# Splitting all feed-forward weights and rotary tables during the first attention, kept in DRAM

## The reference

```python
x1 = x  + attn(layernorm(x), W_Q, W_K, W_V, W_O)      # causal, 16 heads of 64
x2 = x1 + xattn(layernorm(x1), ctx, mask, ...)        # linear attention, 16 heads of 16
y  = layernorm(x2)
for l in range(2):                                    # DEPTH
    h = shift_token(y); q, k, v = split(h @ wqkv[l], 3)      # 8 heads of 64
    q, k = l2norm(q) * q_scale[l], l2norm(k) * k_scale[l]
    q, k = rotary_xpos(q, k)                          # cos, sin and scale tables
    y = y + local_attention(q, k, v) @ wo[l]          # windows of 128
    a, g = split(layernorm(shift_token(y)) @ w1[l] + b1[l], 2)
    y = y + (a * gelu(g)) @ w2[l] + b2[l]             # hidden size 682
out = x2 + y
```

## Time and profile before

| | before |
|---|---|
| median of 3 runs (lowest, highest) | 1203.8 us (1199.09, 1204.12) |
| the profiled execution, its own time | 1201.3 us |
| its span, first to last instruction | 1199.4 us |
| PE busy | 1139.1 us, 95% |
| DVE, ACT, POOL busy | 840.6, 698.7, 591.2 us |
| mean granted TensorE clock | 0.994 |
| DMA | 46.40 MB, 13% of the 16 engines' span |

### The profile page before, as it was taken

How to read it: one execution, slowest core, us unless ns; L and a number is a source line. 1 busy time by engine, 2 the same in 40 slices (tenths; PEclk the granted TensorE clock), 3 DMA queues, 4 the chain that set the end, 5 groups by cost and what they waited for, 6 DMA issues and landing times.

```text
span 1199.4 us, 19590 instructions
## 1 busy us (share of the span) xinstructions
PE 1139.1 (95%) x6624; PEld 886.8 (74%) x6624; DVE 840.6 (70%) x2443; ACT 698.7 (58%) x1696; POOL 591.2 (49%) x649
## 2 busy tenths in 40 slices
PE   5899999999999999997899999999999999999998
PEld 4677777787777766675667787777778778777676
DVE  6788787778777555689988667767675776664541
ACT  3667677777677313562576645657466566574821
POOL 1444444444444311237886654655656646562530
PEclk9899999999999999999999999999999999999999
DMA  7212221212121500010040000000001100002001
GB/s 236 53 37 66 51 48 43 74 42 54 36 54 36 176 18 18 1 62 19 18 134 3 1 1 19 1 1 1 1 18 47 32 1 2 1 5 67 18 1 53
DMA packets 30561, 46.40 MB, mean 39 GB/s; under 512 B 4608, under 2 KB 18304, under 8 KB 30464
## 3 DMA queue, kind: packets, MB, share of 16 engines
q1 hardware_dynamic: 30464, 45.16, 13.1%
HBM read 24.18 MB, written 4.19 MB: 24 GB/s over the span
## 4 chain that ended last, share of the span: by engine, by line
PE 81%; DVE 7%; ACT 4%; DMA 3%; issue 2%; SPq 1%; POOL 1%; DVEq 0%; ACTq 0%; POOLq 0%
PE psum L1495 50%; PE psum L1566 5%; PE psum L1584 5%; PE psum L1716 5%; PE psum L1765 5%; PE psum L1750 4%; PE psum L1732 4%; DMA k<-k_round 2%; PE psum L1698 2%; SPq L592 1%; ACT hnT_hi L969 1%; DVE stats L1041 1%; ACT hnT L969 1%; ACT lp L939 1%; DVE ra L1280 1%
## 5 line engine op out<-in xcount | busy, mean ns | idle before, releaser
L691 POOL TENSOR_TENSOR probs<-probs,rden 128x128 f32<-128x128 f32 (+3 forms) x256 | 176.3, 720 | 211.8 <-DVE rden L1108 211.8
L939 ACT ACTIVATE lp<-lp,lneg,rn 128x256 f32<-128x256 f32 (+1 forms) x256 | 143.8, 572 | 16.5 <-DVE lneg L1336 16.3
L851 ACT ACTIVATE probs<-probs,negmax 128x128 f32<-128x128 f32 (+3 forms) x256 | 140.7, 552 | 15.0 <-DVE negmax L1103 14.4
L1096 DVE CUSTOM_DVE_ANT_0 probs<-psum,causal 128x512 f32<-128x512 f32 (+3 forms) x256 | 110.1, 485 | 23.3 <-PE psum L1495 23.3
L729 POOL TENSOR_TENSOR rn<-ss,neg_half 128x8 f32<-128x8 f32 x64 | 107.5, 1680 | 3.3
L1324 DVE CUSTOM_DVE_ANT_0 lp<-psum,local 128x256 f32<-128x256 f32 (+1 forms) x256 | 83.9, 383 | 20.7 <-PE psum L1716 20.7
L1495 PE MATMUL psum<-q,k_rest 128*128 128x256 f32 (+2 forms) x256 | 86.8, 350 | 9.3 <-DMA k<-k_round 8.7
L720 POOL TENSOR_TENSOR lp<-lp,lrden 128x768 f32<-128x768 f32 x64 | 94.8, 1482 | 0.0
L816 ACT ACTIVATE pT<-psum 128x512 f32<-128x512 f32 (+1 forms) x96 | 49.8, 526 | 76.4 <-PE psum L1566 74.8
L1566 PE MATMUL psum<-ident,probs 128*128 128x128 f32 x640 | 86.1, 274 | 3.1 <-POOL probs L691 2.9
L1495 PE MATMUL psum<-w,hid 124*128 124x256 f32 (+2 forms) x384 | 85.7, 379 | 2.6 <-DVE hid L1400 2.6
(11 more groups left out here) (168 smaller groups left out, 3021.2 us busy)
## 6 DMA issues: line engine op xcount, KB each, us to landing
k<-k_round SPq DMA_DIRECT2D x128, 128.0 KB, 2.4
x<-in_x SPq DMA_DIRECT2D x8, 512.0 KB, 6.3
aw<-in_w_quads SPq DMA_DIRECT2D x4, 768.0 KB, 4.8
w_raw<-in_w SPq DMA_DIRECT2D x2, 1364.0 KB, 6.5
ctxT<-in_ctxT SPq DMA_DIRECT2D x4, 512.0 KB, 7.0
x_scratch<-x SPq DMA_DIRECT2D x4, 512.0 KB, 2.9
x<-x_scratch SPq DMA_DIRECT2D x4, 512.0 KB, 7.0
wqkv_raw<-in_wqkv SPq DMA_DIRECT2D x1, 1536.0 KB, 9.7
```

The costliest lines, as they stand in the source:

```text
L691: ins = pool.tensor_tensor(pr, pr, rden[:, u % 2, h, i:i + 1].broadcast_to([P, TRI[i]]), ALU.mult)
L851: ins = act.activation(pr, pr, ACT.Exp, bias=negmax[:, u % 2, h, i:i + 1], scale=ADH ** -0.5, accum_out=den[:, u % 2, h, i:i + 1])
L939: ins = act.activation(pr, pr, ACT.Exp, bias=lneg[:, u % 2, h, w:w + 1], scale=rn[:, m % 2, w, 0, 2 * j + h:2 * j + h + 1], accum_out=lden ...
L1096: ins = dve.tensor_tensor_reduce(probs[:, u % 2, h, TRI_AT[i]:TRI_AT[i + 1]], bank[:, at:at + TRI[i]], causal[:, S - TRI[i]:S], 1.0, -3e38 ...
```

## The change

- **Weights.** All feed-forward weights (wqkv, w1, w2 with b2 in it, wo) come as one array `w_all`, 8360 columns for each of 128 partitions and each layer, cut into 11 parts of 760 columns: 22 parts in all. During the first attention each part is loaded (`w_raw`, two buffers), rounded by ACT (`w_half`), subtracted by DVE (`w_rest`, in the place of `w_raw`), and both halves are stored to `w_scratch` in DRAM. Parts 2 to 21 take one unit each; parts 0 and 1 stand in START. SP does it behind the copies of k of each unit.
- **Tables.** Both layers' tables are made during units 28 and 29 (ahead of awo.0 and kv.0) and stored; one buffer `tab` is loaded for each layer.
- **Loads.** wqkv and w1 are loaded already split, `lo` and `hi`, straight to where PE reads them. The splits in the entry, in step 0 and at the change of layer are gone, and so are `wqk_next`, `wv_next`.
- **Bias b2.** It is a row of w2, and `hid` has a row of ones for it. POOL's additions of b2 are gone; PE's instructions for w2 keep their number and shape, since that row was there as zeros.
- **The maximum with 1e-24** (L1293 before) is now a `tensor_reduce` over pairs (sum, 1e-24), into a buffer of its own (`ssm`), and the wait for POOL's `l_rn` stands ahead of it, no longer ahead of the sum of squares.
- **Orders.** All token lists are new. In UNIT, PE has `pk` ahead of the second head's scores, and the first head's scores one group of transposes later; ACT's copy of k stands ahead of `t5`.

```diff
-            sp.dma_start(wqkv_raw[:, :, :], a["wqkv"][0].rearrange("(k p) c -> p k c", p=P)).then_inc(ld_wqkv, 16)
+            for c in range(3):
+                layer_wqkv_lo(0, c)
...
+            def load_part(i):
+                l, c = divmod(i, W_PARTS)
+                sp.dma_start(w_raw[:, i % 2, :], a["w_all"][l, :, c * W_PART:(c + 1) * W_PART])\
+                    .then_inc(ld_part[i % 2], 16)
+            def store_part(i):
+                l, c = divmod(i, W_PARTS)
+                sp.wait_ge(part_lo, i + 1)
+                for half, tile in enumerate((w_half, w_rest)):
+                    sp.dma_start(w_dram[l, half, :, c * W_PART:(c + 1) * W_PART], tile[:, i % 2, :].bitcast(F32))\
+                        .then_inc(part_st, 16)
+            load_part(0)
+            load_part(1)
             sp.wait_ge(a_lo, 3)
             quad_weights(1)
...
+                if 0 <= u - 5 < DEPTH * W_PARTS:
+                    store_part(u - 5)
+                    if u - 3 < DEPTH * W_PARTS:
+                        sp.wait_ge(part_st, 2 * 16 * (u - 4))
+                        load_part(u - 3)
...
+            wait_full(sp, plan["awo", B - 1, 1])
+            for c in range(3):
+                layer_wqkv_hi(0, c)
+            wait_read(sp, plan["kv", B - 1, T - 1])
+            layer_tab(0)
...
+            wait_full(sp, plan["k", B - 1, T - 1])
+            layer_wqkv_lo(1, 1)
+            layer_wqkv_hi(1, 1)
+            wait_read(sp, plan["q", B - 1, T - 1])
+            wait_read(sp, plan["k", B - 1, T - 1])
+            layer_tab(1)
...
+            def round_part(i):
+                act.wait_ge(ld_part[i % 2], 16 * (i // 2 + 1))
+                if i >= 2:
+                    act.wait_ge(part_st, 2 * 16 * (i - 1))
+                copy(w_half[:, i % 2, :], w_raw[:, i % 2, :]).then_inc(part_hi, 1)
...
+            def rest_of_part(i):
+                dve.wait_ge(part_hi, i + 1)
+                dve.tensor_tensor(w_rest[:, i % 2, :], w_raw[:, i % 2, :], w_half[:, i % 2, :], ALU.subtract)\
+                    .then_inc(part_lo, 1)
...
-                dve.scalar_tensor_tensor(ss[:, i, :], ss[:, i, :], NORM_EPS ** 2, ss[:, i, :], ALU.max, ALU.max)\
-                    .then_inc(l_ssm, 1)
+                dve.tensor_reduce(ssm[:, i, :], ss[:, i, :, :], AX.X, ALU.max).then_inc(l_ssm, 1)
...
-        UNIT_PE = ("t0 s0@1 t1 t2 s1@1 pk@2 t3 t4 t5 pq@2 z pv@2")
+        UNIT_PE = ("t0 t1 s0@1 t2 pk@2 s1@1 t3 t4 t5 pq@2 z pv@2")
-        UNIT_DVE = ("s0@1 aw2@-1 t0 t2 s1@1 r0@1 t4 pk@2 aw0 pq@2 aw1 r1@1 z")
+        UNIT_DVE = ("aw2@-1 s0@1 t2 t0 s1@1 r0@1 t4 pk@2 aw0 aw1 pq@2 tab@-1 r1@1 z part")
```

More of the change, by code:

```diff
@@ L32 @@
 assert FAT[NF] == HID
+W_SIZE = (E2 * INNER,) * 3 + (E2 * 2 * HID, NF * D, FPAIRS * D)
+W_AT = [sum(W_SIZE[:i]) for i in range(len(W_SIZE) + 1)]
+W_PARTS = 11
+W_PART = W_AT[-1] // W_PARTS
+assert W_PART * W_PARTS == W_AT[-1]
 W = 128
@@ L286, in build @@
         STEPS = DEPTH * B
-        SET1 = 2
+        SET1 = 3
         UNITS = STEPS * FPAIRS
```

291 lines of the change are left out of this document (136 added, 155 removed), and 90 rows, old and new, of tables (CLOSE_DVE, ENTRY_ACT, ENTRY_DVE, ENTRY_PE).

## The result

The changed kernel takes 1208.15 us in the median of four runs (1207.59 to 1208.61), the kernel before beside it 1202.62 (1199.09 to 1204.12): a ratio of 1.0051, with a 95% interval from 1.0032 to 1.0070. It is slower by some 6 us, and lies outside the range of 1180 to 1204. The profiled executions differ in the same way: spans of 1206.3 and 1199.4 us.

The account below looks back on a forecast made before the run. PE was taken as the bound, busy 1139.1 of 1199.4 us, so only its idle 60 us could be won. From 1201.3, -10 + 2 - 5 + 5 - 1.5 - 0.5 = -10 gave 1191 us, range 1180 to 1204.

Parts of the forecast that it names:

- Term 3: First attention, PE's waits for copies of k: copies come earlier in the new unit order, -5 us, bounds 8.7 gained and none.
- margin of 4 us: SP's queue in a unit: SP free again 7.4 us after k_hi, with 11.46 until the next copies of k.
- Rival (c): First attention: SP's wait for the stores takes over the 20 units, 32 us slower, hence 1223; chance 0.08.
- Term 2: First attention: each of 20 units gets an ACT copy and a DVE subtraction, 0.1 us a unit, +2 us, bounds 0 and 10.
- It fits: Attention units: with the new work DVE is busy 9.9 and ACT 9.2 of 11.46 us, so there is room.
- three clean units: First attention: a stretch of 34.38 us with PE busy throughout, 11.46 us a unit, from which DVE's and ACT's load was taken.
- Term 4: Start: the new order puts two statistics and a second normalization ahead of k_rest, delaying the first scores, +5 us.
- Term 1: Entry, 520 to 640 us: DVE loses 15.6 us of work, about PE's idle 15.9, so -10 us, bounds 4 and 14.
- Rival (b): Entry: POOL takes DVE's place as the bound, so the gain there is only 4 us, 1197; chance 0.20.
- over 85%: Sign to look for in the entry: POOL busy for over 85% of its rotary stretch, where it had 44.5 of 55.5 us.
- Terms 5 and 6: Change of layer: splits ahead of hT.5 go, -1.5 us; steps and end: POOL's additions of b2 go, -0.5 us.

Follow-up runs that it names:

- e1: The changed kernel with the load of the next quad's weights, and SP's wait for a_lo, moved behind the stores and the part's load: 1200.4 us.
- e8: The changed kernel with the quad's load and its wait for a_lo between the stores and the next part's load: 1199.0 us.
- e9: The kernel before with the new order of PE, DVE and ACT in a unit, without any part: 1196.6 us.
- e11: The changed kernel with the quad's load last and the old start order, plus a second DVE operation ahead of each of the 22 subtractions: 1222.3 us.
- e2: The changed kernel with PE's, DVE's and ACT's order of the start taken from the kernel before: 1204.2 us.
- e3: The kernel before with only the maximum of the squared norms turned into a reduction over a pair: 1196.8 us.
- e7: The changed kernel with the maximum in its old form, an operation with two tensor inputs on DVE: 1208.8 us.
- e10: The kernel before with the new unit order and the maximum as a reduction, without the traffic through DRAM: 1192.8 us.

## Why the prediction was wrong

**Term 3 failed in what it put at the two new quads, and that is the largest error.** It read: "Only at the two new quads, where the stores queue behind 768 KB and the list of SP stands still until all of it has landed, do the next copies come too late, by about as much as they did". The place was right and the size was not: 8 to 9 us for the two (9.9 in the changed kernel against 0.9 and 1.5 in e1 and e8). What I missed is the wait for `a_lo`, which was there before the change. SP reached it at 115.5 us and left it at 120.9. Before, nothing stood behind it but the next copies of k; now the stores did, and the whole chain of stores, landing and load began 5.4 us late. The queueing behind the 768 KB, which I did name, added 3.3 (6.6 to landing in place of 3.3). How much of the 8 to 9 us each would cost alone was not measured. My margin of 4 us was counted from k_hi, as if SP ran through its list. The second thing missed is ACT: its copy of the part waited 2.04 us for the load, with the exponentials behind it.

The rest of the same term was right. The order of the unit alone is worth 3.8 us in its profile, 3.5 of them in waits for the copies of k as I had said, and 6.4 in the medians (e9); I had 5.

**Rival (c)** named the right mechanism, SP's wait for the stores, but gave it 0.08 and let it act on all 20 units by their landing. The stores landed in 3.3 us in the median, and at the other units the margin that I worked out was there. It decides at single places, through what stands ahead of the stores and not through how fast they are.

**Term 2 was too small:** I took 0.1 us for a unit with a part, 2 us in all; measured are 5.2 to 6.3 us, within the bounds of 0 to 10. The argument that failed is not "It fits". DVE's share was right (9.9 us forecast, 9.86 in the row above), and in ordinary units the price is the 0.1 us that I gave or less. What failed is that three clean units stood for all 20. Where the next quad's weights are split DVE has more to do, and there a part costs up to 1.8 us; the prediction has no term for these three units. Nor was there room for more: e11 pays a second operation in full.

The interference between DVE and POOL, which the prediction weighed there, is real. With POOL at its four products the subtraction takes 1.22 us. At the new quad, where ACT was late and POOL had nearly finished, it took 0.95; and POOL's four products took 3.46 us in the first case and 2.75 in the second (DVE's and POOL's timelines of the changed kernel; POOL's four are one row):

```profile
133.40 0.95 DVE L1278 TENSOR_TENSOR w_rest<-w_raw,w_half 128x760 fp32r<-128x760 f32 x1 [1.98 <-ACT w_half L848]
...
145.49 1.22 DVE L1278 TENSOR_TENSOR w_rest<-w_raw,w_half 128x760 fp32r<-128x760 f32 x1
```

```profile
130.78 2.75 POOL L734 TENSOR_TENSOR probs<-probs,rden 128x128 f32<-128x128 f32 x4 [1.82 <-DVE rden L1128]
...
144.93 3.46 POOL L734 TENSOR_TENSOR probs<-probs,rden 128x128 f32<-128x128 f32 x4 [2.17 <-DVE rden L1128]
```

That is 0.27 us to DVE and 0.7 to POOL for a part. By the rule of the Trainium skill (SBUF — State Buffer, "Who interferes with whom") my estimate had been 0.17 a part and 4 us in all. The rule agrees with these rows. That its 4 us lie nearer to the measured 5.2 to 6.3 than the 2 that I took is luck: it was counted evenly over all parts, and most of them cost nothing.

**Term 4, the start,** had the right sign and reason: forecast +5, bounds 0 and +7, measured +6.7. e2 confirms the order as cause. The end of k_rest, given as 27.8, came out at 28.26, and the scores of unit 1, given as 42, at 42.59.

**Term 1, the entry,** forecast -10 and gave -7.6 (-6.3 to -7.8 over its variants with the reduction). The step that was mis-sized is the addition: 3.5 + 1.6 + 2.5 + 8 us of DVE work for 15.9 us of idle PE. Each half alone wins most of it (e3 4.5, e7 5.6). Rival (b) was near in its reason and off in its size: POOL did come up to 91% of the stretch, as "over 85%" said, and DVE is at 90% (49.99 of 55.54; 52.66 before), so that stretch now has two engines near their full share; but PE idles only 4.8 us in it where it idled 11.1, a gain of 6.2 and not 4. What PE waits for in the entry's second half, from 575 us on, is a row of waits of 0.4 to 1.6 us, most of them for lpT, lmax, lqT and lkT, of both ACT and DVE, whose work this change left as it was.

**Terms 5 and 6** held: -1.5 forecast and 79.78 - 78.33 = 1.45 measured; -0.5 forecast for steps and end and 2.1 - 1.5 = 0.6 measured, less than the scatter of the end.

**The sum by measured sizes** (the parts are what is left of e8's stretch beside the order, so that it must close): start +6.7; new order -4.3 (mean of e9 and e10); parts +5.8 (e8, 1.5 + 4.3); quads +8.4 (e8's 1.5 taken from 9.9); entry -7.6; change of layer -1.5; the rest -0.6. That is +6.9, as the spans differ. The forecast had -10 for the same terms; of the 17 us between, 8.4 are the quads, 3.8 the parts, 2.4 the entry, 1.7 the start and 0.7 the order.

## What to carry to other kernels

Before putting new work into a DMA queue, write down for every wait that the queue already has when it is reached and when it opens; a wait that was harmless because nothing stood behind it costs its whole length once something does. Stores go ahead of such a wait, and loads that nobody waits for soon go last. Work that fits into the ordinary turn of a loop is paid in the turns where the engine has more to do, so look at the fullest turn and not at a clean one. And idle time of an engine inside a loop of several engines is only in part room for work: here one operation went in nearly free and the next cost its whole length. Insert one more of the suspected size and measure before you count on it. Last, try the small parts of a large change alone: here the form of one instruction and the order of a unit give as much as the whole plan with its faults mended.
